# Two score tables for even and odd edge tiles, joined by a maximum on VectorE, in the first graph attention of a long graph network

## The reference, cut to what matters

```python
score = s_src + s_dst + einsum('hed,hd->he', diff, a_dif) \
      + einsum('hed,hd->he', abs(diff), a_abs) + einsum('hed,hd->he', hr_src * hr_dst, a_prd)
alpha = leaky_relu(score)
ex    = exp(alpha.T - segment_max(alpha.T, src)[src])
att   = ex / (segment_sum(ex, src)[src] + EPS)
out   = segment_sum(att[:, :, None] * h_e[:, dst], src)
```

## Time and profile before

| | us |
|---|---|
| median of 3 runs | 2549.97 (2542.49 to 2558.23) |
| the profiled execution | 2558.69 |
| its span | 2556.9 |
| TensorE busy | 2231.5 (87%) |
| VectorE busy | 1093.3 (43%) |
| ScalarE busy | 728.4 (28%) |
| GpSimd busy | 544.3 (21%) |

### The profile page before, as it was taken

The page is one execution under the profiler, slowest core; times in us unless marked ns, Lnnn a source line. Parts: engine busy times, 40 slices in busy tenths (PEclk is TensorE's granted clock), DMA queues, the critical chain, the costliest instruction groups (busy, mean ns, idle before and its releaser), DMA issues.

```text
span 2556.9 us, 22909 instructions
## 1 busy us (share of the span) xinstructions
PE 2231.5 (87%) x7917; PEld 1261.0 (49%) x7917; DVE 1093.3 (43%) x2478; ACT 728.4 (28%) x1206; POOL 544.3 (21%) x474
## 2 busy tenths in 40 slices
PE   6799884888899798878898898899798799999998
PEld 3466553776445443444454454455355354444443
DVE  8796663895333333344362354335334430000002
ACT  1475543775221110002152042124115011111111
POOL 4677732442210100010101101100100220012201
PEclk9899886888999799988899899899899989999999
DMA  9432233311111100022001101100300057777742
GB/s 375 111 57 46 42 100 79 79 40 50 42 52 60 50 11 8 0 106 104 16 1 62 58 0 57 62 0 1 117 29 23 36 199 291 308 289 296 297 187 65
DMA packets 61468, 243.14 MB, mean 95 GB/s; under 512 B 23183, under 2 KB 25699, under 8 KB 39244
## 3 DMA queue, kind: packets, MB, share of 16 engines
q1 hardware_dynamic: 31866, 174.12, 19.3%
q0 software_dynamic: 26336, 62.19, 7.9%
q10 hardware_dynamic: 3168, 5.63, 0.6%
HBM read 209.96 MB, written 31.92 MB: 95 GB/s over the span
## 4 chain that ended last, share of the span: by engine, by line
PE 55%; DVE 16%; issue 16%; POOL 5%; ACT 5%; DMA 3%; PEldq 0%; PEld 0%; DVEq 0%; SPq 0%; POOLq 0%; ACTq 0%
PE PS L724 18%; PE PS L731 10%; PE PS L1221 6%; PE PS L1230 6%; PE PS L1259 6%; POOL pair_scores L1754 2%; DMA pair_scores<-TS,SIDX 2%; DVE ST L1893 1%; POOL pair_sums L1743 1%; PE PS L1020 1%; DVE Y L1901 1%; DVE AR L2184 1%; PE PS L1239 1%; PE PS L769 1%; DVE AR L2165 1%
## 5 line engine op out<-in xcount | busy, mean ns | idle before, releaser
L724 PE MATMUL PS<-XT,WR 128*128 128x113 f32 (+2 forms) x1264 | 364.1, 449 | 9.6 <-ACT XT L1327 7.6
L1725 POOL TENSOR_TENSOR RSTD<-VE,HALF 125x1 f32<-125x1 f32 x105 | 73.6, 701 | 1144.7 <-DVE VE L1896 1144.7
L724 PEld LDWEIGHTS PS<-XT,WR 128*128 128x128 f32 (+1 forms) x1264 | 199.9, 196 | 182.8 <-issue 180.7
L870 PE MATMUL PS<-HR,HOT 125*125 125x512 f32 x800 | 217.8, 422 | 38.0 <-DVE HOT L2041 38.0
L731 PE MATMUL PS<-WR,XT 128*125 128x512 f32 (+1 forms) x480 | 213.6, 598 | 6.5 <-ACT XT L1653 4.3
L2628 DVE TENSOR_TENSOR AR<-AR,PS 128x512 f32<-128x512 f32 (+1 forms) x44 | 30.3, 688 | 405.5 <-PE PS L1230 405.5
L724 PE MATMUL PS<-AR 125*128 125x512 f32 (+3 forms) x680 | 193.5, 439 | 9.3 <-ACT AR L1625 3.9
L870 PEld LDWEIGHTS PS<-HR,HOT 125*125 125x125 f32 x800 | 151.5, 198 | 81.2 <-DVE HOT L2041 30.2
L1918 DVE TENSOR_TENSOR AR<-PS,AR 125x512 f32<-125x512 f32 x55 | 38.0, 692 | 311.9 <-PE PS L731 311.4
L731 PE MATMUL PS<-WR,AR 128*125 128x512 f32 (+1 forms) x370 | 158.5, 580 | 9.9 <-ACT AR L1658 4.6
L724 PEld LDWEIGHTS PS<-AR 125*128 125x128 f32 (+1 forms) x680 | 106.1, 189 | 98.0 <-issue 89.1
(11 more groups left out here) (392 smaller groups left out, 3672.6 us busy)
## 6 DMA issues: line engine op xcount, KB each, us to landing
WR<-in_qkv SPq DMA_DIRECT2D x12, 1024.0 KB
WR<-in_omm SPq DMA_DIRECT2D x12, 1024.0 KB
pair_scores<-CNT SPq DMA_DIRECT2D x1, 12212.0 KB, 55.8
AR<-pair_scores SPq DMA_DIRECT2D x5, 2187.5 KB
AR<-in_x_a SPq DMA_DIRECT2D x10, 1024.0 KB, 9.3
AR<-in_x_b SPq DMA_DIRECT2D x10, 1024.0 KB, 5.1
AR<-in_x_c SPq DMA_DIRECT2D x10, 1024.0 KB, 7.1
WR<-in_x_a SPq DMA_DIRECT2D x8, 1024.0 KB, 9.0
```

Of the source, the lines that this page charges most:

```text
L724: last = mm(s.ap[0:parts, c0:c1], lhs(k), rhs(k)[:, c0:c1], start=(k == 0), stop=(k == terms - 1))
L870: last = mm(DIFF[m % 4], HOT[g % 2][0:P, k, tile(j)], HR[0:P, k, :, b, :], start=(k == 0 and b == 0), stop=(k == NT - 1 and b == 1))
L1725: g.tensor_tensor(RSTD[:, t:t + 1], VE[:, t:t + 1], HALF[:, :], ALU.pow)\
```

## The change

There are two score tables. Even edge tiles are scattered to table 0, odd ones to table 1, and each scatter waits for the one two tiles before. Table 1 is cleared by a second DMA of 12.5 MB that SP issues behind the edge rows of groups 0 to 3; the first scatter to it waits for that. Before the head stage uses a node tile, VectorE takes the elementwise maximum of the two tables: `join`, five pieces of 125 x 1000 numbers a tile. SP loads a tile of table 0 as before, and of table 1 the five pieces (`odd_scores_of`): for tile 0 into five buffers, for tiles 1 to 4 through a ring of two. Tile 0 is joined before the first `raw_scores`; the five joins of tile t + 1 stand one each in steps 8t - 1 to 8t + 3. One of the four `BENT` buffers moves, and some semaphores are merged to make room: `sums_merged` becomes `tables_merged` and counts the joins too, `edge_in` becomes `pieces_in`, `terms_ready` is counted in `start_done`, and the second clear is counted in `stored`.

```diff
-    pair_scores = nc.dram_tensor("pair_scores", [PAIR_ROWS, HEADS0], F32, kind="Internal").ap()
+    pair_scores = [nc.dram_tensor(f"pair_scores_{b}", [PAIR_ROWS, HEADS0], F32, kind="Internal").ap()
+                   for b in range(2)]
...
+        ODD_RING = [view(HR_ + 2 * NT * D + 6250, P, P * HEADS0),
+                    YF[0:P, 3 * D:3 * D + P * HEADS0]]
+        ODD_FIRST = [view(HT_ + P * HEADS0 * q, P, P * HEADS0) for q in range(2)] + [
+            view(HR_ + 2 * NT * D + 5000, P, P * HEADS0)]
+
+        def ODD(t, q):
+            return (ODD_RING + ODD_FIRST)[q] if t == 0 else ODD_RING[q % 2]
+
-        BENT = [view(PT_ + 12250, P, N), BENT_SPARE[:, :]] + [
+        BENT = [FS_ROWS[0:P, 0:N], BENT_SPARE[:, :]] + [
...
+            def clear_scores(b, cleared):
+                sp.dma_start(pair_scores[b].rearrange("(p q) h -> p (q h)", p=128)
+                             .rearrange("p (a q) -> p a q", a=8),
+                             FLAT[0].unsqueeze(1).broadcast_to([128, 8, 3053])).then_inc(cleared, 16)
+
+            clear_scores(0, scores_cleared)
...
             for g in range(4):
                 edge_rows(g)
+            clear_scores(1, stored)
             for g in range(4, GROUPS + 1):
...
+            def odd_scores_of(t, q):
+                rows = pair_scores[1][0:N * N, :].rearrange("(n q d) h -> n q (d h)", n=N, q=NT)
+                for lo, hi in zip(WIDE_ROWS, WIDE_ROWS[1:]):
+                    sp.dma_start(ODD(t, q)[lo:hi], rows[P * t + lo:P * t + hi, q, :])\
+                      .then_inc(pieces_in[q % 2 if t else min(q, 2)], 16)
+
             sp.wait_ge(diff_filled, ET)
-            sp.wait_ge(scattered, 16 * ET)
+            for b in range(2):
+                sp.wait_ge(scattered[b], 16 * ET // 2)
             scores_of(0)
+            sp.wait_ge(tables_merged, NT)
+            sp.wait_ge(graph_filled, 1)
+            for q in range(NT):
+                odd_scores_of(0, q)
             sp.wait_ge(graph_taken, 1)
             scores_of(1)
-            for t in range(2, NT):
-                sp.wait_ge(raw_taken, HEADS0 * (t - 1))
-                scores_of(t)
+            for t in range(1, NT):
+                if t >= 2:
+                    sp.wait_ge(raw_taken, HEADS0 * (t - 1))
+                    scores_of(t)
+                for q in range(NT):
+                    sp.wait_ge(tables_merged, NT + NT * t + max(q - 1, 0))
+                    odd_scores_of(t, q)
...
             def put_scores(m):
 
-                if m:
-                    pool.wait_ge(scattered, 16 * m)
+                if m >= 2:
+                    pool.wait_ge(scattered[m % 2], 16 * (m // 2))
                 else:
-                    pool.wait_ge(scores_cleared, 16)
+                    pool.wait_ge((scores_cleared, stored)[m], 16)
                 pool.wait_ge(score_ready, m + 1)
                 g.indirect_dma_start(
-                    out=pair_scores, out_offset=bass.IndirectOffsetOnAxis(ap=SIDX[:, m:m + 1], axis=0),
-                    in_=TS[:, m % SCORES_AHEAD, :], in_offset=None).then_inc(scattered, 16)
+                    out=pair_scores[m % 2], out_offset=bass.IndirectOffsetOnAxis(ap=SIDX[:, m:m + 1], axis=0),
+                    in_=TS[:, m % SCORES_AHEAD, :], in_offset=None).then_inc(scattered[m % 2], 16)
...
+            def join(j):
+
+                t, q = divmod(j, NT)
+                if t >= NT:
+                    return
+                if q == 0:
+                    dve.wait_ge(pairs_in[t % 2], 32 * (t // 2 + 1))
+                if t == 0:
+                    dve.wait_ge(pieces_in[min(q, 2)], EDGE_PIECES + 32 * (1 if q < 2 else NT - 2))
+                else:
+                    dve.wait_ge(pieces_in[q % 2], EDGE_PIECES + 32 * (1 + (3 - q % 2) * (t - 1) + q // 2 + 1))
+                at = slice(P * HEADS0 * q, P * HEADS0 * (q + 1))
+                v.tensor_tensor(TSC[t % 2][:, at], TSC[t % 2][:, at], ODD(t, q), ALU.max)\
+                 .then_inc(tables_merged, 1)
...
+            for q in range(NT):
+                join(q)
             for k in range(4):
                 raw_scores(k)
                 shift(k)
...
                 if k + 4 < NT * HEADS0:
                     raw_scores(k + 4)
+                if k == 0:
+                    join(NT)
+                if k % HEADS0 == HEADS0 - 1:
+                    join(NT * (t + 2))
+                elif k % HEADS0 < NT - 1:
+                    join(NT * (t + 1) + h + 1)
                 if k + 2 < NT * HEADS0:
                     weighted(k + 2)
```

More of the change, by code:

```diff
@@ L50 @@
 HOTS = 4
+EDGE_PIECES = 16 * 2 * GROUPS // 4
 PARTS = 3
@@ L433, in program @@
         loaded = [sem("weights_in_0"), sem("weights_in_1")]
-        rows_in, edge_in = sem("rows_in"), [sem(f"edge_in_{b}") for b in range(4)]
+        rows_in, pieces_in = sem("rows_in"), [sem(f"edge_or_score_pieces_in_{b}") for b in range(4)]
         modw_in, br_in, mod2_in, br2_in, noise_in = map(sem, ("modw_in", "br_in", "mod2_in", "br2_in", "noise_in"))
@@ L441, in program @@
         uv_ready, hr_split = sem("uv_ready"), sem("hr_split")
-        terms_ready, row_part_ready = sem("terms_ready"), sem("row_part_ready")
+        row_part_ready = sem("row_part_ready")
         ids_in = [sem(f"edge_ids_in_{b}") for b in range(2)]
@@ L446, in program @@
         weighed_ready = sem("weighed_ready")
-        scattered = sem("scores_scattered")
+        scattered = [sem(f"scores_scattered_{b}") for b in range(2)]
         sums_scattered = [sem(f"sums_scattered_{b}") for b in range(2)]
@@ L457, in program @@
         sums_in = sem("pair_sums_in")
-        sums_merged = sem("sums_merged")
+        tables_merged = sem("tables_merged")
         pairs_in = [sem("pair_scores_in_0"), sem("pair_scores_in_1")]
@@ L488, in program @@
         emb_ready, sin_ready = sem("emb_ready"), sem("sin_ready")
-        out_ready, out_done = sem("out_ready"), sem("out_done")
+        out_ready, stored = sem("out_ready"), sem("stored")
         def room_for(eng, m):
@@ L537, in edge_rows @@
                     sp.dma_start(ER[g % 4][lo:hi].rearrange("p a b -> p (a b)"),
-                                 a["edge_attr"][lo:hi, 256 * g:256 * (g + 1)]).then_inc(edge_in[g % 4], 16)
+                                 a["edge_attr"][lo:hi, 256 * g:256 * (g + 1)]).then_inc(pieces_in[g % 4], 16)
             sp.wait_ge(clear_row_ready, 2)
@@ L546, in loads @@
             edge_ids(1)
-            sp.dma_start(pair_scores.rearrange("(p q) h -> p (q h)", p=128)
-                         .rearrange("p (a q) -> p a q", a=8),
-                         FLAT[0].unsqueeze(1).broadcast_to([128, 8, 3053])).then_inc(scores_cleared, 16)
+            def clear_scores(b, cleared):
[3 more added lines that the diff above has]
+            clear_scores(0, scores_cleared)
             for j in range(3):
@@ L577, in loads @@
                 if t:
-                    sp.wait_ge(sums_merged, t)
+                    sp.wait_ge(tables_merged, t)
                 for b in range(2):
@@ L696, in _ @@
                 sp.wait_ge(out_ready, t + 1)
-                sp.dma_start(out[P * t:P * (t + 1), :], X[0:P, t, :]).then_inc(out_done, 16)
-            sp.wait_ge(out_done, 16 * NT)
+                sp.dma_start(out[P * t:P * (t + 1), :], X[0:P, t, :]).then_inc(stored, 16)
+            sp.wait_ge(stored, 16 * (NT + 1))
         @block.tensor
@@ L1403, in _ @@
                     if k == 0:
-                        act.wait_ge(edge_in[g % 4], 32 * (g // 4 + 1))
+                        act.wait_ge(pieces_in[g % 4], 32 * (g // 4 + 1))
                         if g >= PARTS:
@@ L1418, in _ @@
                 magnitude(m)
-            act.wait_ge(sums_merged, NT)
+            act.wait_ge(tables_merged, NT)
             for t in range(NT):
@@ L1732, in _ @@
                 g.tensor_tensor(TERMS[k], wm(0, w), r.unsqueeze(1).broadcast_to([128, K4, D]), ALU.mult)\
-                 .then_inc(terms_ready, 1)
+                 .then_inc(start_done, 1)
             def add_sums(m):
@@ L1774, in counted @@
                 g.tensor_tensor(SP0[k % 4], SP0[k % 4], CNT[:, k // HEADS0, :], ALU.mult).then_inc(counted_ready, 1)
-            pool.wait_ge(sums_merged, NT)
+            pool.wait_ge(tables_merged, NT)
             ahead = signed(0)
@@ L2006, in node_terms @@
             def node_terms(k):
-                dve.wait_ge(terms_ready, k + 1)
+                dve.wait_ge(start_done, 9 + k + 1)
                 step(v.tensor_reduce(UVT[:, k, :], TERMS[k].rearrange("p c (h d) -> p (c h) d", d=DH0),
@@ L2051, in scored @@
                 if m >= SCORES_AHEAD:
-                    dve.wait_ge(scattered, 16 * (m - SCORES_AHEAD + 1))
+                    dve.wait_ge(scattered[m % 2], 16 * ((m - SCORES_AHEAD) // 2 + 1))
                 v.tensor_reduce(TS[0:P, m % SCORES_AHEAD, :], Z[m % 4].rearrange("p (h d) -> p h d", d=DH0),
@@ L2098, in merge @@
                 v.tensor_tensor(CNT[:, t, :], one[:, :, 0], two[:, :, 0], ALU.add)
```

(4 more changed lines are left out.)

2 lines of the change are left out of this document (1 added, 1 removed).

## The result

The changed kernel takes 2562.20 us, the median of 11 runs (2556.41 to 2564.48), against 2549.97 for the kernel before, which also had 11 runs (not the 3 of the table above). The ratio is 1.0044 (95% interval 1.0030 to 1.0057): 11 us slower. The prediction was 2545, 4.6 us faster. So the two profiles alone show no slower kernel at all, and the pair has to be read step by step.

The account below looks back on a forecast made before the run. It took chained score scatters on GpSimd to bound the edge stage and VectorE the head stage. -31 + 12.4 + 14 = -4.6 gave 2554 us from the profiled 2558.69, 2545 against the median; own range 2534 to 2558.

Parts of the forecast that it names:

- -31: Edge stage: with two scatters in flight, the load of tile 0 goes out at 380, not 411; bounds -9 and -43.
- +12.4: Before the head stage: 9 us for table 1's 2.5 MB and 3.4 for three joins of tile 0; range 9 to 15.
- +14: Head stage: the other 20 joins cost 31.6 us of VectorE, somewhat over half taken by gaps; bounds +4 and +32.
- T = 136: Landing time of the second clear, for which put 1 waits; lower bound 132, upper 158.
- 46 us, last score at 377: End of edge stage: first merge to last score shrinks from 52.8 us, as VectorE's 6.7 us of scatter waits go.
- -43: Edge stage: the bound of the gain at the load of tile 0, with T at 132 and a bare step of 3.25.
- six or so are left and end before T, at no cost: Start of edge stage: slow sum scatters beside the second clear, each 9 us beside the first, add nothing.
- 136 + 186: Edge stage: GpSimd's 54 steps at 3.45 us after T end at 322, so the last sum comes 7 us earlier.
- The wait for them shrinks: Head stage: while VectorE joins, TensorE already fills the next raw scores, so VectorE waits less for them.
- rival 2: Head stage: joins cost more, gaps take little, the loop grows by 28; net +9, 2559 us; chance 0.15.
- Rival 1: Edge stage: the clear holds GpSimd; slower from T = 141 on, +17 or 2567 us at T = 158; chance 0.15.
- three signs of being wrong: Put 1 leaving after 145, the tail of puts staying, or joins waiting over 10 us in all for pieces.

Follow-up runs that it names:

- second pair of profiles: Both kernels unaltered, profiled again: the kernel before 2550.66 us, ratio 0.9994; the changed kernel 2562.49 us, ratio 1.0046.
- the kernels without joins: The changed kernel without the joins of node tiles 1 to 4: also without their table 1 loads 2543.05 us, with these loads 2544.08 us.
- the control: Either kernel unaltered, profiled a second time: the kernel before 2550.66 us, ratio 0.9994; the changed kernel 2562.49 us, ratio 1.0046.
- the control of before: The kernel before, unaltered, profiled again: 2550.66 us, ratio 0.9994.
- the spare clear: The kernel before plus a 12.5 MB clear of a table that nothing uses, behind the edge rows of groups 0 to 3: 2572.07 us, ratio 1.0083.
- without later joins: The changed kernel without the joins of node tiles 1 to 4, without their table 1 loads 2543.05 us or with them 2544.08 us.
- joins alone: The changed kernel with all 25 joins but without the loads of table 1 for node tiles 1 to 4: 2563.67 us, ratio 1.0032.

## Why the prediction was wrong

The sum had three terms: -31, +12.4 and +14. The second pair of profiles has -21.9, +13.2 and +22.2, and by the times of the kernels without joins the last is 19.5: -21.9 + 13.2 + 19.5 = +10.8, the 11 us measured. In the first two terms the mechanism was right. In the third it was not: the absorption that the prediction counted on did not come. The errors of the first and the third, 9 and 5.5 us, both to the good side, turn the sign.

**The load of tile 0 31 us earlier: 21.9.** "T = 136" and the step of 3.45 us nearly held: put 1 at 138.4, steps of 3.44. But the term "-31" subtracted from the timeline of one profile, and in that profile the edge stage was 3.2 us late at put 55 and 3.6 late at the load. Put 1 was 2.4 us later than T. Against the control put 55 is 2.1 us earlier, and not 7. A further 3 us are in "46 us, last score at 377": from the first merge to the last score it took 48.8 (52.1 in the control of before), since the waits did not all go. The puts still waited 15.3 us for scatters in all, three of them 3.2, 4.2 and 4.4 us at 330.8, 341.3 and 352.9, beside sum loads issued at 325, 334 and 345. The rule on completion that the prediction drew from the Trainium skill, "DMA: Bandwidth & Descriptors", section on queues, rings and completion order, would have these scatters wait for earlier writes of the load too, and the waits fit it; I applied it to the clear only. No run tells that rule from a plain sharing of the DMA engines. The last part, "the last put leaves at once", held: the last put came 1.4 us after the last score, and the load 2.8 after that. (The bound of -43 is a slip: T at 132 and 54 steps of 3.25 instead of 3.45 give -31 - 4 - 10.8, or -46.)

**The clear.** The prediction put a price on it only through T, and wrote of the slow sums that "six or so are left and end before T, at no cost". They set put 0, 16 us late. In this kernel that happens to end about where the clear does (the rate is 320 GB/s at 137 to 138 us and 120 at 139 to 140), so put 1 stood near the forecast time; the cost of 22 us that the spare clear shows was in the sum, hidden inside "136 + 186". But seen as a term of its own it is half of the overlap's gain, and that would have been the reason to doubt the change.

**The joins of tile 0, +12.4: 13.2** (12.1 in the first profile). Right: 9 us for 2.5 MB more and 3.4 for three joins.

**The other 20 joins, +14: 19.5.** This step failed. Their own time was right (1.19 us against 1.13). Wrong was that the gaps would take part of it ("I let somewhat over half be taken"). With the means of the second pair from 443 to 591 us, a join took 1.83 us (29.2 us for 16), so 36.5 for 20; `weighted` and `shift` fell from 1.27 and 0.58 to 1.01 and 0.35, which gives 19.5 back over 40 steps. So VectorE got 17 us of work on balance, not 31.6, and the time rose by 19.5 (18 by the ratios): little or none of it was absorbed. "The wait for them shrinks" did not come true in the control (14.1 us in 33 heads, then 16.5 in 29; without later joins 8.8 in 33, with joins alone 11.8 in 29), and it did once the join stood behind `shift` (7.6 in 30). This is rival 2's reason, "a join delays `weighted` and so the turn on TensorE", at 19.5 us instead of the 28 that rival 2 named. Whether `weighted` or `shift` is the one that matters, and how much comes by TensorE's clock (last section), was not separated.

**The rivals.** Rival 2, given 0.15, named net +9 and is the nearest. Rival 1 was right that the clear holds GpSimd, but not beyond T = 141. The 80% for "within 1%" held; the forecast's own range, 2534 to 2558, did not.

**The signs.** Most of what the prediction said would show it came: put 1 right behind the clear, steps of 3.4 us, the first merge at 332.5, no tail of puts, VectorE over 90% busy in the first profile (87% in the second). Of its three signs of being wrong one came in the letter, waits for pieces of over 10 us in all (13.2 in the control), but 12.3 of them are at tile 0, where the second 2.5 MB was in the sum. No sign told of the two terms that were too good.

## What to carry to other kernels

A second buffer that takes a wait away has to be filled and emptied: price its clear as a bulk transfer beside whatever small scatters run then, and its join at full length unless a run shows that a gap takes it. Gaps of the bounding engine need not absorb work that is put in front of instructions that others wait for; moving a join behind two of them was worth some 5 to 7 us here. Before a chain of small transfers is overlapped, look for what makes single ones of them slow: here moving five loads of 1.25 MB, and the merges with them, gained 15 to 19 us where the second table lost 11.

And one profile of each kernel carries 3 to 6 us of scatter at an event in the middle: where the terms of a sum are that size, profile the kernel before twice.

## What was not expected of the hardware

A 12.5 MB clear that no instruction waits for slowed the kernel by 19 us. While it ran, at 385 GB/s over 100 to 135 us, scatters of 125 rows that otherwise let the next one go after 0.3 to 1.4 us made it wait up to 6.2; in the changed kernel, at 377 GB/s, up to 7.9.

What VectorE loses beside GpSimd's products is nearly conserved: where a join loses it, the next operations don't. The groups above show it for the join, `weighted` and `shift`: 1778, 1025 and 351 ns against 1193, 1182 and 425 with the join elsewhere.

TensorE's granted clock in the head stage was lower with the joins. A window's mean lies between 1.00 (2.4 GHz) and 0.50 (1.2 GHz): 0.71, 0.82, 0.81 and 0.78 in the four windows from 443 to 591 us of the second profile after, 0.95, 0.86, 0.86 and 0.86 in that of before. TensorE's matmuls recorded there are fewer, 697 against 797, but so are the heads, 29 against 33. The first of these windows, before and after:

```profile
443.00:480.00 37.00, 32.06 (x217) 27.12 (x216) 32.10 (x63) 30.90 (x49) 15.42 (x11) 0.95 0.27 69
...
443.00:480.00 37.00, 34.51 (x183) 29.88 (x182) 27.30 (x53) 24.83 (x39) 12.87 (x9) 0.71 0.51 126
```

At 0.71 TensorE is busy 34.5 of 37 us and VectorE only 27.3, so in this window TensorE is the nearer bound. The first profile after had 0.89 there, with 30.3 and 34.0, and its head steps took 194.0 us instead of 196.9. How much of the 19.5 us comes by the clock was not separated.
